# Matmuls whose result nobody reads, issued by TensorE where it waits: the last batch's cross attention and the start and turn of the feed-forward

## The reference, cut to what matters

```python
x = x + self_attention(layernorm(x))                 # causal, 1024 x 1024 scores per head
x = x + cross_attention(layernorm(x), ctx)           # q from x, k and v from 77 context rows
x = x + feed_forward(layernorm(x))

def feed_forward(x):                                 # 256 -> 704 -> 256, fake-quantised to 8 bits
    xq = act_fake_quant(x, clip_x)                   # scale = sigmoid(clip) * max|x| / 127, over ALL of x
    gate, up = xq @ wq(w_gate).T, xq @ wq(w_up).T
    h = act_fake_quant(silu(gate) * up, clip_down)   # again one maximum over all of h
    return h @ wq(w_down).T
```

## Time and profile before

| | |
|---|---|
| median of 3 runs | 1010.6 us (1007.6 to 1010.87) |
| the profiled execution's own time | 1008.16 us |
| its span in the profile | 1006.4 us |
| mean granted TensorE clock | 0.955 |
| busy, share of the span | TensorE 88%, VectorE 71%, ScalarE 60%, GpSimd 30% |

### The profile page before, as it was taken

How to read it: one execution, slowest core, us unless ns; L and a number is a source line. 1 busy time by engine, 2 the same in 40 slices (tenths; PEclk the granted TensorE clock), 3 DMA queues, 4 the chain that set the end, 5 groups by cost and what they waited for, 6 DMA issues and landing times. The chain is left out here.

```text
span 1006.4 us, 16988 instructions
## 1 busy us (share of the span) xinstructions
PE 890.3 (88%) x5867; PEld 440.3 (44%) x5867; DVE 718.1 (71%) x1477; ACT 602.9 (60%) x1118; POOL 301.0 (30%) x343
## 2 busy tenths in 40 slices
PE   4788899999999899999999898999999867858855
PEld 2424343455544533554445344553445434443334
DVE  3789866768776774787777838777672386778977
ACT  2234577746576577356775764656786524627876
POOL 1242235420421229214231192233411212204510
PEclk9879999999999999999999999999999976978979
DMA  5240111335222142102221233012200612013017
GB/s 161 92 131 20 54 52 56 71 64 80 83 79 65 42 143 80 47 17 78 84 81 44 85 101 85 28 41 94 84 13 23 199 44 91 24 55 133 1 38 255
DMA packets 80063, 76.03 MB, mean 76 GB/s; under 512 B 19324, under 2 KB 74236, under 8 KB 79980
## 3 DMA queue, kind: packets, MB, share of 16 engines
q1 hardware_dynamic: 74908, 71.41, 22.8%
q10 hardware_dynamic: 3456, 2.94, 0.9%
q0 software_dynamic: 1616, 0.58, 0.7%
HBM read 22.43 MB, written 13.13 MB: 35 GB/s over the span
## 5 line engine op out<-in xcount | busy, mean ns | idle before, releaser
L752 ACT ACTIVATE probs<-psum 128x512 f32<-128x512 f32 (+1 forms) x608 | 314.6, 577 | 182.3 <-PE psum L945 179.4
L1119 DVE CUSTOM_DVE_ANT_0 junk<-psum,mask 128x640 bf16<-128x640 f32 (+3 forms) x256 | 253.5, 1022 | 62.9 <-PE psum L909 61.0
L669 POOL TENSOR_SCALAR_AFFINE_SELECT probs<-probs 128x512 f32<-128x512 f32 x128 | 81.3, 638 | 392.6 <-ACT probs L752 392.3
L945 PE MATMUL psum<-q_stack,k_stack 98*128 98x512 bf16 (+3 forms) x768 | 188.7, 332 | 7.9 <-DMA q_stack<-max_rows 2.7
L970 PE MATMUL psum<-probs,v_sb 128*17 128x512 f32 (+3 forms) x1536 | 159.5, 493 | 3.8 <-POOL probs L669 3.4
L1115 DVE TENSOR_REDUCE rowmax<-psum 128x4 f32<-128x512 f32 (+2 forms) x96 | 97.4, 1044 | 62.9 <-PE psum L903 62.5
L909 PE MATMUL psum<-k_stack,q_stack 96*128 96x512 bf16 (+3 forms) x512 | 129.5, 347 | 6.1 <-DVE rowmax L1119 4.8
L945 PEld LDWEIGHTS psum<-q_stack,k_stack 98*128 98x128 bf16 x768 | 63.0, 98 | 138.2 <-ACT probs L752 80.7
L869 PE MATMUL psum<-xnT,wT 128*128 128x512 f32 x192 | 95.4, 630 | 1.6 <-ACT xnT L717 1.5
L796 PE MATMUL psum<-wT,xnT 128*128 128x256 f32 x384 | 90.0, 393 | 2.0 <-ACT xnT L717 1.9
L796 PEld LDWEIGHTS psum<-wT,xnT 128*128 128x128 f32 x384 | 75.1, 198 | 14.3 <-ACT xnT L717 2.3
(11 more groups left out here) (173 smaller groups left out, 1203.3 us busy)
## 6 DMA issues: line engine op xcount, KB each, us to landing
q_stack<-q_parts SPq DMA_DIRECT2D x192, 64.0 KB, 2.6
k_stack<-k_parts SPq DMA_DIRECT2D x192, 64.0 KB, 2.6
xq_stack<-xq_parts SPq DMA_DIRECT2D x168, 64.0 KB, 2.6
xn<-in_x SPq DMA_DIRECT2D x8, 512.0 KB, 4.9
res<-in_x SPq DMA_DIRECT2D x4, 1024.0 KB, 7.1
resid_hbm<-res SPq DMA_DIRECT2D x8, 512.0 KB, 2.6
resid<-resid_hbm SPq DMA_DIRECT2D x8, 512.0 KB, 4.6
out<-o_sb SPq DMA_DIRECT2D x7, 512.0 KB, 3.2
```

Of the source, the lines that this page charges most:

```text
L669: nc.gpsimd.affine_select(out=tile, in_=tile, compare_op=ALU.is_ge, fill=0.0, base=0, pattern=[[0, GH], [1, P]], channel_multiplier=-1).th ...
L752: nc.scalar.activation(probs[n % 2][:, heads * k:heads * k + heads, 0:cols], bank_a(s)[:, 0:heads * cols].rearrange("p (h n) -> p h n", h= ...
L945: last = nc.tensor.matmul(bank[:, cols * n:cols * n + cols], k_stack[:, slot, h, P * j:P * j + P], q_stack[:, slot, half, h, q0 - HALF * h ...
L1119: nc.vector.tensor_tensor_reduce(out=junk[D_STEPS.place(s) % 2][:, 0:keys], in0=bank_d(s)[:, 0:keys], in1=m.mask[:, T - keys:T], scale=1.0 ...
```

## The change

TensorE gets 187 additional matmuls. Each multiplies the 128x128 identity by 512 columns of bfloat16 data and writes PSUM bank 7, which nothing reads afterwards before it is written anew. None of them waits for a semaphore of its own or signals one; each is placed behind one real instruction of TensorE and ahead of the next one, which waits. In `run_layers` a function `fillers(s)` tells how many stand ahead of step s: 142 in all, 118 of them in the last batch's `yT` to `xT` and 24 ahead of `wrow`. In `feed_forward` there are 2 and 12 around the first `over_partitions`, 18 ahead of the second (behind a wait for all silus), then 2 and 11. No other engine's instructions change.

```diff
--- before.py
+++ after.py
@@ -376,6 +376,21 @@
 VALUES, XVALUES = one_of("yN"), one_of("xyN")
 XLOADS, RLOADS, CLOADS = one_of("xload"), one_of("rload"), one_of("cload")
 XMAXES, RSTORES, TSTORES = one_of("xmax"), one_of("rstore"), one_of("tstore")
+
+
+def fillers(s):
+
+    kind, last = s[0], B - 1
+    if kind == "wrow":
+        return 24
+    if kind in ("yT", "o", "xT", "q") and s[2] == last:
+        return {("yT", 0, last, 0, 0): 4, ("o", 0, last, 0): 4, ("o", 0, last, 1): 2, ("xT", 1, last, 0, 0): 5,
+                ("q", 1, last, 0, 0): 3, ("xT", 1, last, 0, 1): 24, ("q", 1, last, 0, 1): 2, ("xT", 2, last, 0, 0): 2}.get(s, 0)
+    if kind == "mT" and s[1:3] == (1, last):
+        return 6 if s[3] < 2 and s[4] == 0 else 2
+    if kind in ("xs1", "xs2", "xy", "xyN") and s[1] == last:
+        return 2 if kind == "xy" or (kind == "xs1" and s[3] % 2 == 0) or (kind == "xs2" and s[4] == 0) else 0
+    return 0
 
 
 def run_layers(nc, m, w):
@@ -799,8 +814,10 @@
                 last.then_inc(d_full, 1)
 
             pe.wait_ge(ident_done, 2)
-            seen = set()
             for s in ORDER:
+
+                for _ in range(fillers(s)):
+                    nc.tensor.matmul(psum[:, 7, :], m.identb[:], m.mask[:, 0:HALF], start=True, stop=True)
                 if s[0] == "kx":
                     c = s[1]
                     if c == 0:
@@ -1277,13 +1294,20 @@
 
         @block.tensor
         def _(pe):
+            def fill(bank, many):
+
+                for _ in range(many):
+                    nc.tensor.matmul(m.psum[:, bank, :], m.identb[:], m.wgT[:, 0, 0:HALF], start=True, stop=True)
+
             def over_partitions(column, n):
 
                 nc.tensor.transpose(m.psum[0:1, 0, 0:P], column, m.ident[:]).then_inc(row_full, 1)
+                fill(7, 2)
                 pe.wait_ge(row_max, n + 1)
                 nc.tensor.matmul(m.psum[:, 1, 0:1], m.ones[0:1, :], small[0:1, TOP], start=True, stop=True).then_inc(spread, 1)
 
             over_partitions(m.xmax[:], 0)
+            fill(7, 12)
             for n in range(NB):
                 pe.wait_ge(xq_done, n + 1)
                 for i in range(FT):
@@ -1300,8 +1324,10 @@
                                                     xq[n % 3][:, c, :], start=(c == 0), stop=(c == CC - 1))
                     last.then_inc(gu_full, 1)
             pe.wait_ge(silu_done, FT * NB)
+            fill(7, 18)
             pe.wait_ge(h_maxed, 1)
             over_partitions(small[:, HLOC], 1)
+            fill(7, 11)
             pe.wait_ge(h_scaled, 1)
 
             def down(n, i, t):
```

## The result

| | before | changed |
|---|---|---|
| median of 20 runs | 1007.88 us | 1002.07 us |
| lowest and highest | 999.33, 1012.78 | 996.77, 1007.05 |
| profiled execution, own time | 1008.16 | 1002.83 |
| its span | 1006.4 | 1001.0 |
| its mean granted clock (1.00 is full speed) | 0.955 | 0.985 |

The ratio is 0.995, interval 0.9932 to 0.9967: faster by half a per cent, 5 to 6 us. Forecast were 999.6 us and 9.8 us gained. The time lies in the range; the gain is little more than half of the forecast one. Runs more than 1.5% above the fastest of their kernel are left out of all ratios and intervals, not of the medians, which takes out three of the six runs of e1 and at most one of any other kernel.

The account below looks back on a forecast made before the run. TensorE at half clock was taken to bound 837.4 to 857.5 us of the tail. Terms -5.2 - 3.0 + 2.7 - 1.9 - 2.1 - 0.3 = -9.8 us gave 998.4 or 1000.8, middle 999.6; range 996 to 1002.5, 8 in 10 994.5 to 1006.5.

Parts of the forecast that it names:

- (a): First `o` of the tail: four added matmuls hidden in a wait, `o` from 5.41 to 3.62 us; -1.8 us.
- (b): `q` on half 0: at full clock VectorE's split starts sooner and has no wait left; -1.7 us.
- (c): `xT` and `q` on half 1: run warm, limited by VectorE's 1.53 us of idle time; -1.5 us.
- (d): Scoring, first half: 17.9 us at half clock become 8.9, plus 5.2 for added matmuls and 0.8 of waits; -3.0 us.
- (e): Scoring, second half: already at full clock, nothing to gain, 28 added matmuls only partly in waits; +2.7 us.
- (f): Last layer norm to the barrier: VectorE's wait for `o` goes, `wrow` and last transposes become about half; -1.9 us.
- (h): Turn in the feed-forward: 18 added matmuls lie in idle time, two short matmuls get faster; -0.3 us.
- (g): First tiles behind the barrier: 12 added matmuls fit idle time, the next twelve matmuls take 2.6 for 5.07; -2.1 us.
- rival 1: Clock still falls at the first `yT`, at 884 and in the turn into the feed-forward; 1005.4 us, chance 0.17.
- Rival 2: Scoring pairs cost nothing, since TensorE's true gaps are longer than the idle times shown; 996 us, chance 0.12.
- Rival 3: Stack transfers issued by SP become the bound, 4.7 us lost; 1004.3 us, chance 0.04.
- Rival 5: Slower: scoring stays at half clock with the pairs in it, first half +8.6 us; 1014.2 us, chance 0.09.

Follow-up runs that it names:

- e1: The changed kernel without the pairs of added matmuls in the scoring loop, the two sixes ahead of mT kept; 0.988 of the kernel before, median 1003.05 us.
- e11: The changed kernel with GpSimd's split of the last q made to wait for VectorE's split on the same half; 0.993 of the kernel before, median 997.54 us.
- e5: The changed kernel with one added matmul in place of each pair in the scoring loop, sixes kept; 0.989 of the kernel before, median 997.07 us.
- e8: The changed kernel with scoring pairs only ahead of xy and mT, first half only, plus e3's edit; 0.989 of the kernel before, median 995.12 us.
- e2: The changed kernel without the 28 added matmuls of the scoring's second half, behind the third xy; 0.991 of the kernel before, median 999.14 us.
- e9: The changed kernel with e5's singles in scoring's first half, none in the second, e3's edit, three more ahead of the last sixteen transposes; 0.991 of the kernel before.
- e6: The changed kernel with the edits of e2 and e3 together; 0.993 of the kernel before, median 999.33 us.
- e7: The changed kernel without the 45 added matmuls of the feed-forward; 0.995 of the kernel before, median 1001.15 us.
- e3: The changed kernel with 4 more added matmuls at the end of run_layers and 4 for 2 behind the first maximum's transpose; 0.993 of the kernel before.
- e4: The changed kernel with all 187 added matmuls over 16 columns instead of 512; 1.001 of the kernel before, median 1009.66 us.
- e10: As e9, but with single added matmuls in the second half of the scoring too; 0.992 of the kernel before, median 996.49 us.

## Why the prediction was right, and where its sizes were off

**(a) and (b) were right.** `o` takes 3.72 us; VectorE's sum comes 1.70 us sooner after its start and the first split 1.52, with 0.17 us of wait left (forecast 1.8 and 1.7, none left). The 24 matmuls ended as the layer norm did: the transposes behind them show no wait at 821.33, where VectorE's `xn` ended at 821.27.

**(c) was right as far as the second split**, which starts 1.60 us sooner (forecast 1.5). The three terms add up to 5.0, not to the 5.2 that the forecast puts into its sum. What follows the split was wrong: from the first `o` the split had gained 4.82 us, the first `xs2` only 4.15. VectorE's third operation of that split takes 0.83 us longer beside GpSimd's, of which e11 gives 0.6 back. I had not seen that GpSimd's split follows ScalarE and would move onto VectorE's. And the step "is not behind them" was wrong: I had the hold-up of 0.4 at the second group's `xs1`, but took the first `xs2` to wait for its transfer alone, while in the changed kernel it comes behind the pairs.

**(d) was right in kind, and 0.6 us too high**, and the larger part of that is the real work. From start to start, the real matmuls of D take 9.4 us in the changed kernel, where I had halved the whole of 17.9 to 8.9. The 24 added ones take 6.1 us with the waits left behind them, where I had 5.2 and 0.8. The step behind a pair starts 0.43 us after it in most places and 0.5 to 0.7 ahead of `xy` and `mT`, so that TensorE still waits a little there although the profile shows it busy for 15.38 of 15.50 us. e5 and e8 show that 12 matmuls in place of 24 do the same, with D at 13.6: the twelve that e5 leaves out saved 1.9 us of the 2.6 that they stream. Five other kernels with the changed kernel's code there took 15.3 us, so 0.2 of the 0.6 may be chance.

**(e) had the loss right and 0.7 us too small.** Its 28 matmuls cost 3.40 us. By e5 fourteen cost 1.3 (27.55 less 26.26), the second fourteen 2.1, or 0.09 and 0.15 us each of 0.217: of a single one more lies in a wait than of the second of a pair. That they would buy nothing there I had said; e2 shows it. e8 and e9, with nothing added there either, lost 1.7 us to a fall.

**(f) and (h) were right**, 1.86 for 1.9 and 0.4 for 0.3. VectorE's wait for `o`, 0.92 us before, is gone.

**(g) is the step that failed most**, 0.90 for 2.1. I took the clock to hold across the barrier; it fell, as rival 1 said for this place: the twelve took 4.45 us and the gate came 1.14 us later than before (5.95 us behind the barrier's transpose against 4.81; rival 1 had it 1 late). Rival 1 had the gates gain nothing beside that. They ran at full clock, and so 0.90 is left of the gain. With the clock up, G is 15.10 and the term 2.06, as forecast.

The sum of the misses is 1.05 in A, 0.6 in D, 0.7 in E and 1.2 in G, that is 3.5 of 9.8.

**Some of the nearness is luck.** By the medians the gain is 5.8 us and 4.0 too small, yet the time is off by 2.5 only. The forecast set out from 1009.4 us (999.6 and 9.8), between the profiled execution and a median of three runs; the median of twenty is 1007.88. That start, 1.5 too high, covered so much of the miss.

**The rivals.** Rival 1 came true at one of its three places in the changed kernel. At the second, the transposes at 884, the clock fell in e1, e6 and e7. Near the first it fell in e2 and e3, but was back ahead of `o`. Rival 2 fell with E at 29.67, though part of its premise shows: the record of two matmuls of 512 columns is 0.59 us long while such twos start 0.43 apart (904.00, 904.43 and 904.86 in the changed kernel), so it runs 0.16 past the start of the next. Rival 3 fell: the first `xs2` of the changed kernel shows no wait for a transfer. Rival 4 is what e4 is, not this kernel. Rival 5 fell, as D is 15.52 and not 26.5. But what spoke for it was true: e1's 23 us at 0.50 with TensorE busy 22.07 are the same as the earlier trace rows showed. In the changed kernel the clock never fell ahead of the loop, so its trace doesn't tell whether added matmuls raise a fallen clock. Other traces bear on it: in e2, e3 and e10 the clock fell near 833 and was back by 836.8, ahead of the first `xs2`, while e1's, with no pairs to follow, fell at 835.9 and stayed down for 27 us. No run puts this to the test by itself.

**Of the transposes.** Two added matmuls among the sixteen transposes stand in the changed kernel and in ten of the others (e4's are thin). Eight of these eleven traces ran the place without a fall, although transposes prevail there; e1, e6 and e7 did not. Two of the eight, e9 and e10, have three more just ahead. The fall at 885 isn't the last before the barrier, as the prediction has it: 895.2 to 901.7 in the earlier trace rows follows, over the wait of 6.36 us. The runs do not show that transposes bring the clock down: e7 has the changed kernel's program up to the barrier, and yet F is 17.64 in the one and 16.26 in the other.

**What stays open.** The fall behind the barrier is in the changed kernel, e2 and e11 and not in e1 and e5, which have the same code there; the five kernels with e3's edit never have it. That this edit is what holds the clock is likely by these counts and not shown. What decides over the falls near 833 and 859 is as open. No run tried added matmuls at the wait of 1.65 us alone, behind which e8 and e9 lost 1.7 us. Whether e5, e8 or e9 is the best version is open too; all three have a shorter tail than the changed kernel by 5 us. So is how often the clock holds in e1's loop without pairs.

## What to carry to other kernels

Matmuls that nobody reads can pay where the clock falls behind TensorE's waits, as it did here behind two of 1.18 and 1.13 us, and the work behind them is TensorE's own. Their length counts: with 512 columns each the clock of the changed kernel stayed at 1.00 from the first `o` on but for one fall, and with 16 (e4) it fell where it had fallen before. Best each lies in a wait; one that doesn't is paid for, up to 0.217 us at full clock here, and must cost less than the clock it saves. Work out their price per place, and try the half of them first: one ahead of each wait held the clock as well as two here, and the loop was 4.1 us shorter, beside 6.3 us that the whole change took from the tail. Where the clock holds without them, as in the second half of this loop in e2 and e6, they only cost, 3.40 us for the 28 of the changed kernel.

Measure such a change by distances within the trace. The 20 runs of the kernel before lie 13.45 us apart, or 1.3%, and this change is half a per cent.

## What the runs showed of the hardware

- **A fallen clock stayed down under load.** It stood at 0.50 for 20 us with TensorE busy 89% before, and for 23.33 us with 95% in e1. Other falls ended sooner, some with TensorE busy throughout (899.8 to 903.9 in the changed kernel), one with it busy for 2.93 of 6.50 us (895.2 to 901.7 before). The rows don't tell why.
- **Falls came behind short waits, and longer waits passed without one.** Ahead of the fall at 799.5 before the change the waits were 1.18 and 1.13 us. In the last 6 us ahead of e1's at 835.9 none was longer than 0.52. In e2 and e3 the clock fell behind a wait of 1.97 us, and in e8 and e9 behind one of 1.65; the changed kernel has the first of these and e2 the second, and neither fell there.
- **Under the same code the clock fell in one execution and not in another.** The changed kernel and e7 have the same program up to the barrier, and only e7's clock fell at the sixteen transposes. From the first `o` on, and where full added matmuls stand, it fell near 833 in e2, e3 and e10, near 859 in e8 and e9, at the sixteen transposes in e1, e6 and e7, behind the barrier in the changed kernel, e2 and e11, and near 914 in e8 and e11.
- **The scatter of the times went with the clock's.** Over 23 runs of the kernel before, from 998.23 us at a mean clock of 0.962 to 1015.35 at 0.943, time and mean clock have a correlation of -0.94, at 0.8 us for 0.001. Over the 20 runs of the changed kernel it is -0.85, from 996.77 at 0.990 to 1007.05 at 0.980. Over the seven runs of e11, which lie 2.5 us apart, it doesn't show.
- **VectorE and GpSimd slowed each other down.** A subtraction over 128x512 took VectorE 1.52 us beside GpSimd's and 0.69 alone, and GpSimd's took 1.40 beside it and 1.15 in e11. From the start of GpSimd's at 828.23 to the end of VectorE's at 830.18 it was 1.95 us, and the two take 1.84 apart. How they share is not shown.
